# A two-layer model: the attention's fourth mask and context moved, its values projected once, two state-space projections moved, and another order at the end of the last feed-forward

## The chip, the cores and the metric

One core of one Trainium2 chip runs the whole program as one launch. The metric is the device time of one execution in microseconds (us), lower is better. TensorE is called PE here, its weight loads PEld; VectorE is DVE, ScalarE is ACT, GpSimd is POOL, and SyncE (SP) only issues DMAs.

## The reference

An input x of 2 sequences x 1024 tokens x 128 features passes through six blocks, each `x = x + block(layernorm(x))`, the feed-forwards with a factor 0.5 before the block:

1. a gated feed-forward (128 to 512 to 128, ReLU), scaled by the normalised top-two gates of 8;
2. windowed attention: 16 heads of 8 features, token i sees the tokens i-63 to i of its sequence; softmax over them, then an output projection with bias;
3. the gated feed-forward again;
4. a feed-forward with ternary weights and GELU, whose hidden rows are divided by their root mean square;
5. a selective state-space layer: in-projection to 2 x 256 channels, causal convolution over 4 tokens, SiLU, projections to delta, B and C, then for each channel and each of 16 states the recurrence h = exp(delta*a)*h + delta*u*B, y = sum of C*h, gated and projected out;
6. the ternary feed-forward again.

All data is fp32; a mask and some selector matrices are bf16.

## The kernel before, in words

Tokens are handled in 4 chunks of 512 (`NC`), each of 4 tiles of 128 (`TPC`), so 16 tiles (`NT`). Each engine runs a list of instructions written out by hand, in that order, and waits on counting semaphores. There is no planner: the order in the file is the order on the engine. The stages follow each other on the time axis: gated feed-forward (to 45 us), attention (45 to about 190 us), gated and ternary feed-forward (to about 262 us), state space (to about 500 us), ternary feed-forward `ter1` (to the end).

**Attention** (`attn_tensor`, `attn_vector`, `attn_scalar`). The heads are 4 groups of 4 (`j`). For tile t PE computes the scores of all four groups into four PSUM banks (`scores`, L683, 64 instructions). Each bank is first filled with the mask by a product with an identity (`mask_scores`, L671, one 512-column bf16 product), and the scores are added onto it. DVE takes each group's maximum (L566) and subtracts it (L571): that is `soften(t, j)`. ACT takes the exponent in place (`probs`, L836). PE transposes the four heads of the group (`prob_t`, L696). ACT copies the transposes out of PSUM (`probs_t`, L842), and PE multiplies them with the values (`values`, L710; the values carry a column of ones, so that the row sum comes with it). DVE divides by the row sum (`context`, L576 and L580), PE transposes the result (`context_t`, L736), ACT copies it (`copy_ctx`, L848), PE projects it (`project`, L740), and DVE adds it to x (`update`, L587). The work on tile t-1's context stands inside tile t. On PE one tile reads: transpose group 0, transpose the context of t-1, transpose group 1, project t-1, masks 0 and 1 of t+1, transpose group 2, masks 2 and 3, scores of t+1, values of groups 0 and 1, transpose group 3, values of groups 2 and 3.

The products of the next chunk are spread over tiles i = 1, 2, 3 of the chunk before: the transposes of x and the queries (L643, L648) in tile 1, the keys (L653) in tile 2. A window of the values begins every 64 tokens and is 128 tokens long, so each token's values are needed at two partition positions; the kernel projects them twice (`project_v(c, p)`, L663, eight instructions a call, two calls a chunk, one in tile 2 and one in tile 3), and ACT copies both (L830). For this, xw holds 64 tokens of the chunk before in front of the 512.

**State space** (`ssm2_*`). 64 steps k = 16 states x 4 units (sequence, half of the channels). In each step PE spreads B over the partitions (`spread_B`, L1173, into banks 2 and 3), DVE multiplies by delta*u (L1026), ACT makes exp(delta*a) (L1281), DVE runs the scan over 1024 tokens (L1047, three buffers hst), POOL multiplies with C (L1123, four buffers hC), and PE adds that onto y (`add_state`, L1193, five steps behind). Every fourth step (k % 4 = 3, but for the last one of units 1 and 2) POOL does DVE's product instead (L1107). `dt_proj(i)` (L1140) makes the delta of unit i; units 1 to 3 use banks 2 and 3, so nothing can be spread there until ACT has copied the result out (`take_z`). A softplus follows later, between two loads of ACT's function table.

**Ternary feed-forward** (`Ffn` ter0 and ter1). Per chunk: four up blocks (L441), GELU on each (L520), then four squares (L533), four down blocks (L447). POOL adds the four squares up (`ffn_pool`, L416 twice and L420), PE sums over the partitions (`token_sums`, L494, behind the up blocks of the next chunk, for the last chunk behind its own down blocks), DVE and POOL make the root (L375, L424, L380, L381) and DVE adds the scaled output to x (`update`, L389). The output leaves by one DMA a chunk.

## Time and profile before

| what | us |
|---|---|
| median of 3 timed executions | 553.44 (549.71 to 555.21) |
| the profiled execution | 548.81 |
| its span in the profile | 547.1 |
| PE busy | 476.1 (87%) |
| DVE busy | 440.7 (81%) |
| POOL busy | 305.2 (56%) |
| ACT busy | 273.0 (50%) |

The profile is one execution: 1.7 us lie around its span, and it stands 4.6 us under the median. Its times count from the start of the span. The granted clock (PEclk) is given as a share of 2.4 GHz, so 0.5 means 1.2 GHz. In a chain row a duration is the time by which the instruction moved the chain on.

### The profile page before, as it was taken

How to read it: one execution, taken by the hardware profiler on the slowest of the kernel's cores; microseconds unless marked ns; L12 is line 12 of the kernel's file. 1: busy time of each engine (PE TensorE's matmuls, PEld its weight loads, DVE VectorE, ACT ScalarE, POOL GpSimd, SP SyncE). 2: the span in 40 equal slices, each digit the busy share in tenths (PEclk: the TensorE clock that was granted, in tenths of full speed). 3: DMA queues.
4: the chain of work that ended last, by engine and by line, in shares of the span. 5: the costliest groups of instructions: out<-in, count | busy, mean ns of one | idle time of the engine just before them, and what ended most of it. 6: DMA issues, size and time to landing. Idle time of an engine off the chain costs nothing.

```text
span 547.1 us, 10120 instructions
## 1 busy us (share of the span) xinstructions
PE 476.1 (87%) x3876; PEld 290.8 (53%) x3876; DVE 440.7 (81%) x889; ACT 273.0 (50%) x420; POOL 305.2 (56%) x229
## 2 busy tenths in 40 slices
PE   7999899989899989999787889987667777889994
PEld 3876677777776777777331333333223233336764
DVE  4678768687769567667978988899999999998653
ACT  2345656565656524666786537344443434331742
POOL 3348200203000011567425888999999999993574
PEclk9999998999989899999896788989999998999998
DMA  8000000000000000000009843344553345100011
GB/s 218 5 0 3 4 2 1 2 3 4 1 2 3 2 0 2 2 0 2 0 31 416 340 154 154 143 166 166 218 230 155 154 192 206 62 1 0 2 39 40
DMA packets 12323, 42.74 MB, mean 78 GB/s; under 512 B 2858, under 2 KB 8755, under 8 KB 10227
## 3 DMA queue, kind: packets, MB, share of 16 engines
q1 hardware_dynamic: 11458, 41.56, 19.9%
q8 instruction: 31, 0.51, 0.4%
q10 hardware_dynamic: 816, 0.53, 0.3%
q14 instruction: 18, 0.14, 0.1%
HBM read 40.78 MB, written 1.31 MB: 77 GB/s over the span
## 4 chain that ended last, share of the span: by engine, by line
PE 44%; DVE 25%; issue 13%; POOL 8%; ACT 8%; DMA 1%; POOLq 0%; DVEq 0%; ACTq 0%
DVE hst L1047 10%; PE bk L447 6%; PE bk L441 6%; PE bk L710 5%; PE bk L696 5%; PE bk L1193 5%; PE bk L683 3%; ACT bk L1281 3%; DVE dBu L1026 3%; DVE xnT L278 3%; POOL hC L1123 3%; PE bk L671 2%; ACT g L842 2%; PE bk L931 2%; POOL powers L292 1%
## 5 line engine op out<-in xcount | busy, mean ns | idle before, releaser
L1123 POOL TENSOR_TENSOR hC<-hst,rows 128x1024 f32<-128x1024 f32 x62 | 144.7, 2359 | 14.8 <-DVE hst L1047 12.3
L1047 DVE TENSOR_TENSOR_SCAN hst<-bk,dBu 128x1024 f32<-128x1024 f32 x64 | 144.5, 2274 | 1.0 <-POOL dBu L1107 0.9
L1193 PE MATMUL bk<-hC,ident 128*128 128x512 f32 x256 | 127.6, 634 | 2.5 <-ACT ysb L1271 1.6
L1281 ACT ACTIVATE bk<-delta,aneg 128x1024 f32<-128x1024 f32 x64 | 71.5, 1118 | 100.2 <-DVE hst L1047 100.2
L285 POOL TENSOR_TENSOR veps<-mv,lneps 128x4 f32<-128x4 f32 x24 | 5.7, 239 | 159.2 <-DVE mv L257 159.1
L1193 PEld LDWEIGHTS bk<-hC,ident 128*128 128x128 f32 x256 | 51.3, 203 | 55.3 <-issue 41.5
L520 ACT ACTIVATE rows<-bk 128x512 f32<-128x512 f32 x64 | 38.1, 597 | 60.5 <-PE bk L441 60.5
L566 DVE TENSOR_REDUCE smax<-bk 128x4 f32<-128x512 f32 x64 | 43.7, 682 | 25.5 <-PE bk L683 25.5
L1026 DVE TENSOR_TENSOR dBu<-bk,du 128x1024 f32<-128x1024 f32 x50 | 59.9, 1198 | 5.2 <-PE bk L1173 5.2
L1173 PE MATMUL bk<-s,sel 96*128 96x512 bf16 x100 | 31.6, 398 | 35.7 <-DVE dBu L1026 33.3
L842 ACT COPY g<-bk 128x512 f32<-128x512 f32 x64 | 37.4, 585 | 47.0 <-PE bk L696 46.4
L1173 PEld LDWEIGHTS bk<-s,sel 96*128 96x128 bf16 x100 | 7.6, 100 | 74.1 <-DVE dBu L1026 58.3
L571 DVE TENSOR_TENSOR g<-bk,smax 128x512 f32<-128x512 f32 x64 | 44.2, 691 | 2.2
L836 ACT ACTIVATE g<-g 128x512 f32<-128x512 f32 x64 | 40.8, 638 | 8.4 <-DVE g L571 7.7
L696 PE MATMUL bk<-ident,g 128*128 128x128 f32 x256 | 42.2, 292 | 2.0 <-ACT g L836 2.0
L710 PE MATMUL bk<-rows,g 128*64 128x9 f32 x1024 | 38.1, 205 | 1.6
L710 PEld LDWEIGHTS bk<-rows,g 128*64 128x64 f32 x1024 | 33.7, 138 | 9.6 <-issue 5.1
L696 PEld LDWEIGHTS bk<-ident,g 128*128 128x128 f32 x256 | 31.1, 148 | 9.9 <-ACT g L836 5.1
L1107 POOL TENSOR_TENSOR dBu<-rows,du 128x1024 f32<-128x1024 f32 x14 | 33.0, 2357 | 0.0
L292 POOL TENSOR_TENSOR powers<-veps,lnpow 128x4 f32<-128x4 f32 (+1 forms) x24 | 30.1, 1255 | 1.9
L447 PE MATMUL bk<-wmoe,rows 128*128 128x128 f32 x256 | 30.3, 275 | 0.0
L441 PE MATMUL bk<-xnT,wmoe 128*128 128x512 f32 x64 | 30.2, 608 | 0.0
(174 smaller groups left out, 757.4 us busy)
## 6 DMA issues: line engine op xcount, KB each, us to landing
rows<-c_rows SPq DMA_DIRECT2D x16, 2048.0 KB, 7.1
rows<-c_rows SPq DMA_DIRECT2D x4, 1024.0 KB, 9.6
x<-in_x_dram SPq DMA_DIRECT2D x4, 256.0 KB, 4.9
out_dram<-x SPq DMA_DIRECT2D x4, 256.0 KB, 2.3
wmoe<-in_w_dram ACTq DMA_DIRECT2D x2, 256.0 KB, 5.3
wup<-in_upT_dram SPq DMA_DIRECT2D x1, 256.0 KB
wdn<-in_downT_dram SPq DMA_DIRECT2D x1, 256.0 KB
wproj<-in_in_wT_dram SPq DMA_DIRECT2D x1, 256.0 KB
```

What stands on the lines that cost most here:

```text
L441: nc.tensor.matmul(bank[k][:, :], f.w_up[:, k * P:(k + 1) * P], xT[:, :], start=True, stop=True).then_inc(f.up, 1)
L447: last = nc.tensor.matmul(psD[c % 2][:, i * P:(i + 1) * P], hT[:, k, i * P:(i + 1) * P], f.w_down[:, k, :], start=(k == 0 and i == 0), sto ...
L566: nc.vector.tensor_reduce(smax[:, j * HPG:(j + 1) * HPG], s3d, AX.X, ALU.max).then_inc(at["max"], 1)
L571: nc.vector.tensor_tensor(ssub[:, j, :].rearrange("p (a k) -> p a k", a=HPG), s3d, m, ALU.subtract).then_inc(at["sub"], 1)
L696: last = nc.tensor.transpose(psPT[j % 2][:, a * P:(a + 1) * P], ssub[:, j, a * P:(a + 1) * P], ident[:, :])
L710: last = nc.tensor.matmul(psO[64 * s:64 * s + 64, h, :], pT[:, j, a * P + 64 * s:a * P + 64 * s + 64], va[:, t // TPC % 2, 2 * (t % TPC) + ...
L842: nc.scalar.copy(pT[:, j, :], psPT[j % 2]).then_inc(at["pts"], 1)
L1026: nc.vector.tensor_tensor(dBu[k % 3][:, :], bk23[:, :], du[k // NS % 2][:, :], ALU.mult).then_inc(m2["dBu"], 1)
L1047: nc.vector.tensor_tensor_scan(hst[k % 3][:, :], dA[k % 2][:, :], dBu[k % 3][:, :], 0.0, ALU.mult, ALU.add).then_inc(m2["scan"], 1)
L1123: nc.gpsimd.tensor_tensor(hC[k % 4][:, :], hst[k % 3][:, :], crep[:, k % 12, :], ALU.mult).then_inc(m2["hC"], 1)
L1193: last = nc.tensor.matmul(bk01[:, r * CH:(r + 1) * CH], ident[:, :], hC[k % 4][:, r * CH:(r + 1) * CH], start=(k % NS == 0), stop=(k % NS ...
L1281: nc.scalar.activation(dA[k % 2][:, :], delta[:, i, :], ACT.Exp, scale=aneg[:, h * NS + n:h * NS + n + 1]).then_inc(m2["dA"], 1)
```

## The change

It has four parts.

**1. Order of the attention.** The mask of group 3 is multiplied in behind the scores (`mask_behind`, its own semaphore `masked`, which only DVE's group 3 waits for); the scores open that bank themselves. `scores` now waits for all four groups of the tile before. DVE's `context(t-1)` stands behind `soften(t, 2)` and not before it; on PE `context_t` stands behind masks 0 and 1, `project` behind the transposes of group 2; ACT's `copy_ctx` stands behind the exponent of group 2.

**2. Values once per token.** One `project_v(c)` and one copy a chunk write the odd windows of va; SP copies them by DMA from SBUF to SBUF into the even windows, two DMAs for chunks 0 and 2 and three for chunks 1 and 3, and `values` waits for them. xw loses its 64 tokens in front, with ACT's copy of them.

**3. Delta projections.** They stand at steps 0, 7, 19 and 27 instead of 0, 7, 11 and 15. For four steps behind each, `add_state` runs one step later, and is caught up with in step 11, 23 or 31. Softplus 2 moves from step 12 to step 28.

**4. End.** In both ternary feed-forwards each square follows its GELU, into two alternating buffers. For the last chunk of ter1 DVE adds the squares, not POOL, and PE takes the token sums before the last down block.

```diff
-        hsq = home(2048, KB, CH)
+        hsq2 = [home(2048, KB, CH), home(4608, KB, CH)]
...
+        def last_pair(dve, f, k):
+            hsq = hsq2[(NC - 1) % 2]
+            dve.wait_ge(f.hsq, (NC - 1) * KB + k + 2)
+            nc.vector.tensor_tensor(hsq[:, k, :], hsq[:, k, :], hsq[:, k + 1, :], ALU.add).then_inc(f.last, 1)
...
+        def shift_values(sp, c):
+            b = c % 2
+            sp.wait_ge(at["free"], 4 * c + 4)
+            sp.dma_start(va[64:128, b, 0:2 * TPC:2, :, :], va[0:64, b, 1:2 * TPC:2, :, :]).then_inc(v_shift[b], 16)
+            sp.dma_start(va[0:64, b, 2:2 * TPC:2, :, :], va[64:128, b, 1:2 * TPC - 1:2, :, :]).then_inc(v_shift[b], 16)
+            if b == 1:
+                sp.dma_start(va[0:64, b, 0:1, :, :], va[64:128, 0, 2 * TPC - 1:2 * TPC, :, :]).then_inc(v_shift[b], 16)
...
                 soften(t, 1)
+                soften(t, 2)
                 if t > 0:
                     context(t - 1)
-                soften(t, 2)
...
+                if t > 0:
+                    pe.wait_ge(at["sub"], t * JG)
-                pe.wait_ge(at["free"], 5 * c + 3)
+                pe.wait_ge(at["free"], 4 * c + 3)
...
                 last.then_inc(at["s"], 1)
+                mask_behind(t)
...
                 if ahead and i == 3:
-                    project_v(c + 1, 1)
+                    project_v(c + 1)
                 prob_t(t, 0)
-                if t > 0:
-                    context_t(t - 1)
                 prob_t(t, 1)
-                if t > 0:
-                    project(t - 1)
                 if t + 1 < NT:
                     mask_scores(t + 1, 0)
                     mask_scores(t + 1, 1)
                 if t == NT - 1:
                     expert_up(0)
+                if t > 0:
+                    context_t(t - 1)
                 prob_t(t, 2)
+                if t > 0:
+                    project(t - 1)
                 if ahead and i == 1:
                     project_q(c + 1)
-                if ahead and i == 2:
-                    project_v(c + 1, 0)
                 if t + 1 < NT:
                     mask_scores(t + 1, 2)
-                    mask_scores(t + 1, 3)
                     scores(t + 1)
...
+                probs(t, 2)
                 if t > 0:
                     copy_ctx(t - 1)
-                probs(t, 2)
...
+        Z_STEP = [0, 7, NS + 3, NS + 11]
...
+            def sums_to(k):
+                return max(0, k + 1 - LAG) - any(z <= k < z + 4 for z in Z_STEP[1:])
...
-                if k in (7, 11, 15):
-                    dt_proj(k // 4)
-                if k in (8, 12, 16):
-                    add_state(k - LAG - 1)
-                if k >= LAG and k not in (7, 11, 15):
-                    add_state(k - LAG)
+                if k in Z_STEP[1:]:
+                    dt_proj(Z_STEP.index(k))
+                for e in range(sums_to(k - 1), sums_to(k)):
+                    add_state(e)
...
                     if k == 12:
                         softplus(1)
+                    else:
                         softplus(2)
-                    else:
                         softplus(3)
...
                 for k in range(KB):
+                    if f is ter1 and c == NC - 1 and k == KB - 1:
+                        token_sums(c)
                     last = down_block(pe, f, c, k)
...
             for c in range(NC):
-                ffn_pool(pool, ter1, c)
+                if c < NC - 1:
+                    ffn_pool(pool, ter1, c)
```

In the last chunk's turn on DVE, the first `last_pair` stands before the mean of chunk 2, the second one and the total behind chunk 2's root and before chunk 2's update of x.

## Rows read from the trace of the kernel before

**Rows 1.** The attention as one stretch: length, busy of the engines (instructions), PEclk, DMA.

```profile
core 0: us, PE busy (x) PEld busy (x) DVE busy (x) ACT busy (x) POOL busy (x), PEclk, DMA share, GB/s
45.00:190.00 145.00, 133.52 (x2512) 103.39 (x2511) 109.24 (x241) 85.36 (x168) 27.64 (x27) 0.96 0.01 3
```

**Rows 2.** Chain that ended last, scores of tiles 9 to 14: start, us, what.

```profile
123.92 1.14 PE bk L683 x63
...
133.14 1.14 PE bk L683 x62
...
142.72 1.14 PE bk L683 x63
...
151.44 1.14 PE bk L683 x63
...
160.16 1.14 PE bk L683 x63
...
167.99 1.14 PE bk L683 x63
```

**Rows 3.** Timeline of tile 14: start, us, engine, line, operation [idle before].

```profile
172.11 0.26 DVE L576 RECIPROCAL rden<-bk 128x16 f32<-128x16 f32 x1 [0.21 <-PE bk L710]
...
172.61 0.68 DVE L566 TENSOR_REDUCE smax<-bk 128x4 f32<-128x512 f32 x1
172.69 0.59 ACT L842 COPY g<-bk 128x512 f32<-128x512 f32 x1
...
174.05 0.63 ACT L836 ACTIVATE g<-g 128x512 f32<-128x512 f32 x1 [0.61 <-DVE g L571]
...
174.65 0.69 DVE L571 TENSOR_TENSOR g<-bk,smax 128x512 f32<-128x512 f32 x1
174.73 0.42 PEld L696 LDWEIGHTS bk<-ident,g 128*128 128x128 f32 x4 [0.81 <-ACT g L836]
...
175.75 1.21 PE L683 MATMUL bk<-delta,rows 32*64 32x128 f32 x64
```

**Rows 4.** Chain through tiles 10 and 11: values, and values again.

```profile
141.40 0.89 PE bk L663 x8
...
146.79 1.09 PE bk L663 x8
```

**Rows 5.** A stretch of 5 us in tile 12, columns as in rows 1.

```profile
155.00:160.00 5.00, 4.90 (x35) 3.52 (x35) 3.67 (x8) 3.86 (x8) 0.00 (x0) 0.66 0.00 0
```

**Rows 6.** DMA issues: KB each, us to landing.

```profile
out_dram<-x SPq DMA_DIRECT2D x4, 256.0 KB, 2.3
```

**Rows 7.** Costliest groups on the page, then DVE's timeline in the first unit.

```profile
L1026 DVE TENSOR_TENSOR dBu<-bk,du 128x1024 f32<-128x1024 f32 x50 | 59.9, 1198 | 5.2 <-PE bk L1173 5.2
...
318.63 1.22 DVE L1026 TENSOR_TENSOR dBu<-bk,du 128x1024 f32<-128x1024 f32 x1 [1.80 <-PE bk L1173]
```

**Rows 8.** Timeline of the scan stage, PE in step 8, then POOL and DVE in unit 1.

```profile
312.87 5.29 PE L1193 MATMUL bk<-hC,ident 128*128 128x512 f32 x8
...
362.20 2.35 POOL L1123 TENSOR_TENSOR hC<-hst,rows 128x1024 f32<-128x1024 f32 x1 [0.54 <-DVE hst L1047]
...
378.35 2.36 POOL L1107 TENSOR_TENSOR dBu<-rows,du 128x1024 f32<-128x1024 f32 x1
...
380.76 2.28 DVE L1047 TENSOR_TENSOR_SCAN hst<-bk,dBu 128x1024 f32<-128x1024 f32 x1
```

**Rows 9.** Timeline of the last chunk of ter1.

```profile
531.96 0.60 ACT L520 ACTIVATE rows<-bk 128x512 f32<-128x512 f32 x1 [3.85 <-PE bk L441]
...
535.03 2.18 ACT L533 ACTIVATE rows<-rows 128x512 f32<-128x512 f32 x4
...
536.61 1.24 DVE L380 TENSOR_SCALAR gz<-gz 128x4 f32<-128x4 f32 x1 [1.13 <-POOL gz L424]
...
540.45 1.05 PE L494 MATMUL bk<-ones,rows 128*128 128x1 f32 x8 [1.49 <-POOL rows L420]
...
542.84 0.17 DVE L380 TENSOR_SCALAR gz<-gz 128x4 f32<-128x4 f32 x1 [1.13 <-POOL gz L424]
...
543.25 1.12 DVE L389 SCALAR_TENSOR_TENSOR x<-bk,gs,x 128x128 f32<-128x128 f32 x4
```

More of the change, by code:

```diff
@@ L171, in macaron_kernel @@
         out_done = sem("out_done")
+        v_shift = [sem(f"v_shift{q}") for q in range(2)]
         def layer_norm_semaphores(name, ternary=False):
@@ L198, in __init__ @@
                     self.sq = sem(name + "_sq")
+                    self.last = sem(name + "_last")
                     self.ssum = sem(name + "_ssum")
@@ L396, in ffn_vector @@
                     advance_two(dve, n, following, c)
+                    if f is ter1 and c == NC - 2:
+                        last_pair(dve, f, 0)
                     mean_square(c)
@@ L400, in ffn_vector @@
                     rms(c)
+                    if f is ter1 and c == NC - 2:
+                        last_pair(dve, f, 2)
+                        last_total(dve, f)
                 elif begun and c == 0:
@@ L411, in ffn_vector, with last_total @@
                     ternary_weights(dve, 0)
+        def last_pair(dve, f, k):
+            hsq = hsq2[(NC - 1) % 2]
+            dve.wait_ge(f.hsq, (NC - 1) * KB + k + 2)
+            nc.vector.tensor_tensor(hsq[:, k, :], hsq[:, k, :], hsq[:, k + 1, :], ALU.add).then_inc(f.last, 1)
+        def last_total(dve, f):
+            hsq = hsq2[(NC - 1) % 2]
+            dve.wait_ge(f.last, 2)
+            dve.wait_ge(f.ssq, NC - 1)
+            nc.vector.tensor_tensor(ssum[:, :], hsq[:, 0, :], hsq[:, 2, :], ALU.add).then_inc(f.ssum, 1)
         def ffn_pool(pool, f, c):
+            hsq = hsq2[c % 2]
             for k in range(0, KB, 2):
@@ L508, in ffn_tensor @@
                 ahead(pe)
-            if f.ternary:
+            if f is ter0:
                 token_sums(NC - 1)
@@ L527, in ffn_scalar @@
                     take_up(act, f, c, k)
-                if f.ternary:
-                    if c > 0:
-                        act.wait_ge(f.ssum, c)
-                    for k in range(KB):
+                    if f.ternary:
+                        if c > 1:
+                            act.wait_ge(f.ssum, c - 1)
                         act.wait_ge(f.h, c * KB + k + 1)
-                        nc.scalar.activation(hsq[:, k, :], hT[:, k, :], ACT.Square).then_inc(f.hsq, 1)
+                        nc.scalar.activation(hsq2[c % 2][:, k, :], hT[:, k, :], ACT.Square).then_inc(f.hsq, 1)
                 if c + 1 < NC:
@@ L626, in take_first @@
             act.wait_ge(at["xpose"], 1)
-            nc.scalar.copy(xw[:, 0, 64:64 + CH], psT).then_inc(at["free"], 1)
+            nc.scalar.copy(xw[:, 0, :], psT).then_inc(at["free"], 1)
         def attn_first(pe):
@@ L673, in mask_scores, with mask_behind @@
                                  start=True, stop=False, skip_group_check=True)
+            def mask_behind(t):
+                first = int(t % TPB == 0)
+                nc.tensor.matmul(bank[JG - 1][:, :].rearrange("p (a k) -> p a k", a=HPG), identb[:, :],
+                                 mask1[:, first:first + 1, :].to_broadcast([P, HPG, P]),
+                                 start=False, stop=True, skip_group_check=True).then_inc(at["masked"], 1)
             def scores(t):
                 c, b, r = t // TPC, t // TPB, t % TPB
-                pe.wait_ge(at["free"], 5 * c + 3)
+                if t > 0:
+                    pe.wait_ge(at["sub"], t * JG)
+                pe.wait_ge(at["free"], 4 * c + 3)
                 if c > 0:
@@ L685, in scores @@
                                                     kT[32 * j:32 * j + 32, b, r * P + 64 * s:r * P + 64 * s + P],
-                                                    start=False, stop=True, skip_group_check=True)
+                                                    start=(j == JG - 1 and a == 0), stop=(j < JG - 1), skip_group_check=True)
                 last.then_inc(at["s"], 1)
+                mask_behind(t)
             def prob_t(t, j):
@@ L742, in attn_tensor @@
             pe.wait_ge(set_attn, 1)
-            for j in range(JG):
-                if j == 3:
-                    pe.wait_ge(at["free"], 3)
+            for j in range(JG - 1):
                 mask_scores(0, j)
             scores(0)
-            project_v(0, 0)
-            project_v(0, 1)
+            project_v(0)
             for t in range(NT):
@@ L880, in attn_scalar @@
                     take_q(c + 1)
-                if ahead and i == 2:
-                    take_v(c + 1, 0)
                 if t == 0:
@@ L1308, in ssm2_scalar @@
                         softplus(1)
+                    else:
                         softplus(2)
-                    else:
                         softplus(3)
@@ L1363, in _ @@
                 sp.dma_start(dst, src).then_inc(w_in, 16)
+            for c in range(NC):
+                shift_values(sp, c)
             def rows_out(b):
```

81 lines of the change are left out of this document (38 added, 43 removed).

## The prediction

> **What bounds the kernel now.** I read the page's busy shares first (PE 87%, DVE 81%, in the table above): no engine bounds the whole. In the attention PE is busy for 133.5 of 145 us, DVE for 109, ACT for 85 [rows 1]. Then the chain that ended last. It runs over PE through the attention, over DVE's scans from 290 to 494 us, and over short steps that alternate between DVE, POOL and PE in the last 50 us. So each part of the change meets another bound, and I cost each in its own stage.
>
> In the attention the chain gives a tile's length, scores to scores: 9.22, 9.58 and 8.72 us for tiles 9, 10 and 11, which carry work of the next chunk, and 7.83 us for tile 13, which carries none [rows 2]. The timeline of tile 14, another without such work, tells why it isn't shorter: DVE takes the context of tile 13 (with a wait of 0.21 us) before group 2's maximum at 172.61; so ACT stands idle 0.61 us before group 2's exponent at 174.05, PE idles 0.81 us before the transposes at 174.73, and two masks later come the scores at 175.75 [rows 3]. In the scan stage DVE is dense but for 5.2 us of waits for PE's spread of B [rows 7]. At the end everything waits for POOL's last addition of squares [rows 9].
>
> **Attention, order.** The instructions stay, four masks a tile too; they move. Context costs DVE 0.50 us (172.11 to 172.61), and with its wait 0.7 us go from before group 2. The exponent can't use all of it: ACT copies group 0's transposes until 173.28 [rows 3], and the mask that now stands behind the scores pushes these transposes back by half of what two masks take, 0.2 us. So the exponent starts at 173.5 instead of 174.05. Then PE does group 2's transposes (174.2 to 174.6), the projection that has moved behind them (0.4), one mask (0.2), and the scores at 175.25: 0.5 us a tile. DVE's group 3, whose subtraction ended at 175.34 [rows 3], ends 0.3 us earlier and doesn't hold them up. What is late next is PE itself, without a gap from group 2's transposes on, so the fourth mask behind the scores gains nothing by itself: it leaves the path before the scores and enters that behind them. The bounds are 0 (the old chain over ACT holds) and 0.7 us (all that context took). Six tiles carry nothing of a next chunk (0, 4, 8, 12, 13, 14): 3.0 us.
>
> In tiles 1, 5 and 9 ACT also copies the transposed x and PE projects the queries; both stay, only the context's copy leaves the place before group 2's exponent. I take 0.2 us each, 0.6 us.
>
> **Attention, values.** In tiles 2, 6 and 10 PE projects the keys at the start and half of the values (0.89 us) just before the last masks, where the chain runs over it [rows 4]. The second leaves: 0.9 us each, 2.7 us. In tiles 3, 7 and 11 the other half, 1.09 us [rows 4], is replaced by the whole chunk's, again eight instructions; the new order gains little, since ACT's copy of the values and of group 0 stand before group 2's exponent: 0.1 us for the three. ACT loses four copies and two small ones, on no path.
>
> The price is ten DMAs from SBUF to SBUF, at most 144 KB each. The trace has none such. Its nearest row is the output's, 256 KB in pieces of 512 B: 2.3 us from issue to landing [rows 6]. Here the pieces are 576 B, three in a row at most, so 2.3 to 7 us. SP has nothing else to do in this stage. The first use, `values` of a chunk's first tile, stands behind the scores of its second tile: for chunk 0 some 4 us after ACT's copy (two DMAs, 2.3 to 4.6 us), for the others over 8 us. I take 0, and at most 1 us for chunk 0. Were they late, everything on PE behind `values` would wait, the next scores last.
>
> By the Trainium skill ("DMA: Bandwidth & Descriptors", section "Anatomy of one DMA") the fixed part is about 2.0 us, and these bytes add about 0.3 us at the rate it gives; the row of 2.3 us fits that, and the term stays 0.
>
> Attention: 3.0 + 0.6 + 2.7 + 0.1 = 6.4 us, between 0 and 9.
>
> **Delta projections.** Where one stands now, PE spreads B once and then catches up with two `add_state`, 8 instructions in 5.29 us [rows 8]; the next spread comes late and DVE waits 1.80 us at 318.63 [rows 7]. There are three such places, so about 3 us of the 5.2 are left for the two others; I take 1.8 and 1.2 us. After the change only one `add_state` follows in steps 8 and 9, and the two together fall in step 11, where POOL does the product and PE has no spread to make. I keep 0.3 us of the wait, since PE was at 1.2 GHz there (its first four instructions take about 3.4 us). So DVE gets 1.5 + 1.8 + 1.2 = 4.5 us ahead by step 17. POOL follows DVE only until step 12 and then works without a gap (product with C, next unit's delta*u, the product of step 15, and so on), so it gains the first two, 3.3 us, and falls 1.2 us back against DVE. This lag is the new wait: in step 20 POOL idled 0.54 us [rows 8], which takes up a part, but in step 27 POOL's product ended at 380.71 and the scan that needs it began at 380.76 [rows 8]. There DVE loses 1.2 - 0.54 - 0.05 = 0.6 us. Remaining: 4.5 - 0.6 = 3.9 us, which is POOL's pace.
>
> The projections at 19 and 27 stand where POOL does the product too, with the same catch-up, and I cost them at 0: the cover is a scan of 2.28 us [rows 8] on either side. If it is gone, each costs up to 1.8 us. Two softpluses now follow step 28, where one did; exponent 29 then comes later by one softplus, at most the 1.2 us that DVE needs for as many elements [rows 7]; two spread products and two scans of DVE lie between the exponents of 28 and the scan of 29, so 0 again. Scan stage: 3.9 us, between 0 and 5.2.
>
> **The ternary parts.** In ter0 and the first chunks of ter1, POOL starts on the squares only when its own roots are done, after the squares have ended; their interleaving and second buffer gain nothing. It costs nothing either: GELU 3 ends about 1.2 us later (two instructions of 0.6 us a block on ACT), still before the fourth down block. 0.
>
> In the last chunk GELU 0 starts at 531.96; four pairs of GELU (0.60) and square (2.18 / 4 = 0.55 [rows 9]) and 0.05 us between them end at 536.8, not 537.2. DVE makes the root of chunk 2 at 536.61. It took 1.24 us then, against 0.17 us at 542.84 when POOL added nothing [rows 9]; without POOL's additions I take 0.17. So the second addition starts at 537.1. An addition of 512 elements is half of L1026's 1.2 us [rows 7], so two take 1.3 us: the total is there at 538.45, where it was at 540.45 with PE's sums. PE is between down blocks 2 and 3 then. From the sums to the update it stays 543.25 - 540.45 = 2.8 us [rows 9]; the update starts at 541.3. The fourth down block (0.9 us) and chunk 2's update fit in between. 1.9 us, between 0.9 and 2.2.
>
> By the Trainium skill ("SBUF — State Buffer", section "Who interferes with whom") DVE and GpSimd share one pair of ports, which the first comer holds for its whole instruction. The row of 1.24 us agrees. If instead that instruction were simply slow there, the end would gain 0.9 us.
>
> **Sum.** 6.4 + 3.9 + 1.9 = 12.2 us. The profiled execution goes from 548.8 to 536.6 us. The median stands 4.6 us above it; on the median 553.4 - 12.2 = 541.2, and I predict 541 us.
>
> **Rivals.**
>
> *Forecast, 541 us (536.5 to 544.5).* Chance 0.54.
>
> *Attention held by ACT's queue.* PE waits for ACT in every tile; group 2's exponent now goes before the context's copy, so `project` and all behind it may wait for that copy. For it: 0.81 us of PE's idle time in tile 14 is ACT's [rows 3]. Against it: ACT is busy 59% of the attention [rows 1]. The order then gains 0 and the removed values stay: 2.7 for 6.4 us, 545 us. Chance 0.12.
>
> *The scan's waits only move.* PE's pieces now fall at steps 19 and 27, where DVE has no gap at all, and POOL's margin was 0.1 us. If each costs 1.8 us, the stage gains 0.3 us: 545 us. Chance 0.12.
>
> *The clock comes back.* The attention's mean clock of 0.96 [rows 1] means that PE had 1.2 GHz for some 12 us (145 x 0.04 / 0.5). Part of it lies in tile 12 (0.66 from 155 to 160 us, so 3.4 us of it) [rows 5], a bare tile that took 8.72 us, where tile 13 took 7.83 [rows 2]: 0.9 us for 3.4, about 2.5 for all, since some of it fell on PE's waits. Fewer gaps, no stretch: 2.5 us more, 538.5 us. The Trainium skill ("TensorE: Matmul & The Clock Gate", Part 1) has the throttled state as the default, which activity releases; that speaks for this case and against the next. Chance 0.15.
>
> *The clock goes: slower.* One mechanism: `values`, `context_t` and `project` now wait close together in PE's list, and if the clock falls there, PE has no slack left to hide it: each us at 1.2 GHz costs 0.5 us. Before, some 12 us ran so. From 25 us more on all 12.2 us are gone; 40 us more cost 20 us, and the time is 561 us. Against it: PE gets denser. Chance 0.07.
>
> **How the numbers follow.** The range, 534.5 to 547, holds the first four and the spread of the runs shown (5.5 us). A measurement of this kernel can tell about 1% from no change; 1% faster is 547.9 us, beyond the second and third case. Faster: 0.54 + 0.15 + most of 0.24 = 0.87; within 1%: 0.07; slower: 0.06.
>
> **What would show it.** Bare tiles of 7.3 us and tile 10 at 8.7 us; DVE's waits for the spread under 1 us in the first unit, one for POOL near step 27; PE's last token sums at 2 us after the last GELU's square, with a down block behind them. Wrong would be: `values` waiting on a DMA in more than the first tile, waits of DVE at steps 20 or 28, or bare tiles still near 7.8 us.

## The result, and the profile after

Against the kernel before in the same comparison the changed kernel took 544.64 us (541.96 to 549.32, 4 runs) for 554.33 (549.71 to 555.26, 4 runs): a ratio of 0.9891 with a 95% interval of [0.9842, 0.9940]. In the first round of experiments it was run again, 543.42 us for 551.68, ratio 0.9853 [0.9819, 0.9888]. So it is faster by 1.1 to 1.5%, 6 to 8 us, where 12.2 were forecast. The medians themselves lie 9.7 and 8.3 us apart; the text goes by the recorded ratios and their intervals.

The two profiled executions hardly differ, 549.32 us now for 548.81, and one thing has to be taken off before they are compared: the granted TensorE clock. Over the whole span its mean was 0.936 in this execution, 0.945 to 0.948 in the three others (541.96 to 544.76 us). The 23 later runs of the kernel before, one program, lie between 0.955 (548.72 us) and 0.937 (554.29 us): 0.01 of mean clock goes with some 3 us.

First the attention: windows of the changed kernel, columns as in rows 1, and the same stretch in the kernel with the attention's parts alone (second fence), which does the same work there.

```profile
45.00:190.00 145.00, 136.39 (x2473) 104.83 (x2474) 108.82 (x242) 81.78 (x165) 29.48 (x30) 0.92 0.04 10
350.00:355.00 5.00, 3.85 (x8) 1.57 (x7) 5.00 (x4) 3.15 (x3) 5.00 (x3) 0.65 1.01 383
355.00:360.00 5.00, 5.00 (x10) 1.72 (x9) 4.15 (x3) 0.27 (x1) 3.58 (x3) 0.67 0.09 36
530.00:535.00 5.00, 5.00 (x25) 4.13 (x25) 1.35 (x6) 0.57 (x1) 2.53 (x3) 0.76 0.17 52
```

```profile
45.00:190.00 145.00, 136.33 (x2542) 104.43 (x2540) 110.47 (x250) 83.88 (x168) 29.42 (x30) 0.98 0.04 10
```

0.92 and 0.98, where rows 1 have 0.96. The tiles show what that is worth. PE's timeline of the changed kernel, tile 4 and then tile 13, both bare (without work of a next chunk):

```profile
80.39 1.21 PE L719 MATMUL bk<-delta,rows 32*64 32x128 f32 x64
81.53 0.39 PE L705 MATMUL bk<-rows,identb 128*128 128x512 bf16 x1
81.84 1.10 PE L748 MATMUL bk<-rows,g 128*64 128x9 f32 x32
82.88 0.66 PE L733 MATMUL bk<-ident,g 128*128 128x128 f32 x4
83.47 1.38 PE L748 MATMUL bk<-rows,g 128*64 128x9 f32 x32
84.78 1.59 PE L733 MATMUL bk<-ident,g 128*128 128x128 f32 x8
86.17 1.06 PE L699 MATMUL bk<-rows,identb 128*128 128x512 bf16 x2
...
88.89 1.21 PE L719 MATMUL bk<-delta,rows 32*64 32x128 f32 x64
...
164.02 1.21 PE L719 MATMUL bk<-delta,rows 32*64 32x128 f32 x64
...
167.10 1.38 PE L748 MATMUL bk<-rows,g 128*64 128x9 f32 x32
168.41 1.13 PE L733 MATMUL bk<-ident,g 128*128 128x128 f32 x8
169.38 0.59 PE L699 MATMUL bk<-rows,identb 128*128 128x512 bf16 x2
...
171.30 1.21 PE L719 MATMUL bk<-delta,rows 32*64 32x128 f32 x64
```

Tile 13 takes 171.30 - 164.02 = 7.28 us, and PE's only idle time in it is 0.11 us; before it was 7.83 [rows 2]. Tile 4 takes 88.89 - 80.39 = 8.50 us: from 85 us on every product of PE takes nearly double (two masks 1.06 us for 0.59), for some 3.5 us. Seven tiles of this execution have such a stretch (4, 6, 7, 8, 10, 11, 12), each 1.2 to 1.4 us longer than its like at full clock. In the profile before there were two in the same tiles (4 and 12), for 0.74 and 0.89 us, and a third behind them, at 180.2 us. That ate the attention's gain in this profile: from the first scores to those of tile 15 it took 131.5 us for 130.2. All seven begin at the same place: as the second run of 32 products of nine columns ends (84.78 here). The number is that of one execution: six other profiles with the same order on PE have 2, 3, 3, 7, 8 and 9 stretches in the attention. The place is not: of the 61 stretches between 45 and 185 us in all 17 profiles, 60 begin within 0.45 us of the end of such a second run.

The transfers that shift the values, a group of DMA issues on the page (KB each, us to landing), and DVE's first wait in a tile:

```profile
rows<-rows SPq DMA_DIRECT2D x4, 144.0 KB, 2.5
...
rows<-rows SPq DMA_DIRECT2D x4, 108.0 KB, 2.3
```

```profile
L598 DVE TENSOR_REDUCE smax<-bk 128x4 f32<-128x512 f32 x64 | 43.6, 682 | 9.8 <-PE bk L719 9.7
```

Nobody waits for the transfers, and DVE's wait for the scores fell from 25.5 us to 9.7.

The scan stage. DVE's timeline: the first scan, two of the new waits, the last product with y (before, the last product began at 499.32 and the first scan at 292.24):

```profile
294.69 2.29 DVE L1075 TENSOR_TENSOR_SCAN hst<-bk,dBu 128x1024 f32<-128x1024 f32 x1
...
357.57 1.23 DVE L1054 TENSOR_TENSOR dBu<-bk,du 128x1024 f32<-128x1024 f32 x1 [0.85 <-PE bk L1201]
...
367.61 1.23 DVE L1054 TENSOR_TENSOR dBu<-bk,du 128x1024 f32<-128x1024 f32 x1 [1.12 <-PE bk L1201]
...
500.12 1.23 DVE L1097 TENSOR_TENSOR g<-bk,g 128x1024 f32<-128x1024 f32 x1 [1.12 <-PE bk L1221]
```

From the first scan to that last product it took 205.43 us for 207.08. The waits of rows 7 are gone (17th scan 50.9 us behind the first, for 55.5: 4.6 us ahead, 4.5 forecast), and a third new one of 0.63 us for POOL stands at 381.58, as forecast (0.6). The two above were not forecast. PE and ACT there:

```profile
349.15 1.95 PE L1168 MATMUL bk<-wmoe,wdt 9*128 9x512 f32 x4 [1.08 <-DVE dBu L1054]
...
352.25 1.01 PE L1201 MATMUL bk<-s,sel 96*128 96x512 bf16 x2 [1.15 <-issue]
353.06 3.62 PE L1221 MATMUL bk<-hC,ident 128*128 128x512 f32 x4
356.47 1.06 PE L1201 MATMUL bk<-s,sel 96*128 96x512 bf16 x2
357.32 2.37 PE L1221 MATMUL bk<-hC,ident 128*128 128x512 f32 x4
...
360.89 5.39 PE L1221 MATMUL bk<-hC,ident 128*128 128x512 f32 x12 [0.76 <-ACT ysb L1300]
```

```profile
359.73 1.01 ACT L1300 COPY ysb<-bk 128x1024 f32<-128x1024 f32 x1 [5.13 <-PE bk L1221]
```

Step 19 has the projection (1.95 us) between two idle times of 1.08 and 1.15 us; then PE is at 1.2 GHz for 7 us (0.65 and 0.67 in the windows above), an `add_state` takes 3.62 us for 1.88, the next spread is late, and the copy of y of unit 0 waits 5.13 us for the last sum, which now comes a step later. The wait of 1.12 us came at full clock: once y was copied, PE had three sums in a row (5.39 us from 360.89) and `add_skip` (1.02 us) ahead of the spread.

The end. Timeline of the last chunk, GELU and squares on ACT, root and second addition on DVE, sums on PE, update:

```profile
534.42 0.60 ACT L541 ACTIVATE rows<-bk 128x512 f32<-128x512 f32 x1 [5.48 <-PE bk L460]
...
538.74 0.63 ACT L553 ACTIVATE rows<-rows 128x512 f32<-128x512 f32 x1
```

```profile
539.08 0.17 DVE L382 TENSOR_SCALAR gz<-gz 128x4 f32<-128x4 f32 x1 [1.13 <-POOL gz L443]
...
539.49 0.69 DVE L423 TENSOR_TENSOR rows<-rows 128x512 f32<-128x512 f32 x1
540.22 0.69 DVE L429 TENSOR_TENSOR rows<-rows 128x512 f32<-128x512 f32 x1
...
543.76 1.13 DVE L391 SCALAR_TENSOR_TENSOR x<-bk,gs,x 128x128 f32<-128x128 f32 x4
```

```profile
540.96 1.05 PE L515 MATMUL bk<-ones,rows 128*128 128x1 f32 x8 [0.43 <-DVE rows L429]
```

From the first GELU to the update it is 543.76 - 534.42 = 9.34 us, for 543.25 - 531.96 = 11.29 [rows 9]: 1.95 us shorter, 1.9 forecast. Most of it doesn't show in the span because a stretch at 1.2 GHz fell on PE just ahead (0.76 in the last window), which cost 1.6 us: 32 products of the down blocks of chunk 2 took 5.37 us, for 3.74 in the kernel with the end alone. All 13 profiles with this part show 9.33 or 9.34 us from that GELU to the update, the other four 11.28 to 11.30; in six of the 13 the stage behind the last product with y is 1.6 us longer than in the seven others, as here.

### The profile page after: what moved, and what is told of

Read it like the earlier page. It is cut to its first block, busy times and chain, and to the rows that moved or that the text cites. A ratio compares the mean times of both kernels' runs of the same rounds, so it can differ in the third digit from the quotient of the medians.

```text
span 547.6 us, 10085 instructions
## 1 busy us (share of the span) xinstructions
PE 482.3 (88%) x3844; PEld 293.9 (54%) x3844; DVE 441.5 (81%) x892; ACT 268.8 (49%) x414; POOL 301.6 (55%) x225
## 4 chain that ended last, share of the span: by engine, by line
PE 45%; DVE 22%; issue 14%; POOL 10%; ACT 7%; DMA 1%; POOLq 0%; DVEq 0%; ACTq 0%
DVE hst L1075 8%; PE bk L466 6%; PE bk L733 6%; PE bk L460 6%; PE bk L748 5%; PE bk L1221 5%; POOL hC L1151 4%; PE bk L719 3%; DVE xnT L280 3%; ACT bk L1310 3%; DVE dBu L1054 3%; POOL powers L294 2%; ACT g L871 2%; DVE stats L255 1%; POOL dBu L1135 1%
## 5 line engine op out<-in xcount | busy, mean ns | idle before, releaser
L1221 PE MATMUL bk<-hC,ident 128*128 128x512 f32 x256 | 125.1, 623 | 2.7 <-ACT ysb L1300 1.8
L1201 PE MATMUL bk<-s,sel 96*128 96x512 bf16 x100 | 33.4, 419 | 33.3 <-DVE dBu L1054 30.7
L733 PE MATMUL bk<-ident,g 128*128 128x128 f32 x256 | 44.2, 313 | 7.0 <-ACT g L865 6.9
L733 PEld LDWEIGHTS bk<-ident,g 128*128 128x128 f32 x256 | 33.0, 159 | 16.0 <-ACT g L865 12.0
L865 ACT ACTIVATE g<-g 128x512 f32<-128x512 f32 x64 | 39.2, 636 | 1.3 <-DVE g L603 1.3
L466 PE MATMUL bk<-wdn,rows 128*128 128x128 f32 x256 | 31.8, 285 | 0.0
L460 PE MATMUL bk<-xnT,wmoe 128*128 128x512 f32 x64 | 31.6, 631 | 0.0
```

The lines of the kernel that those rows point to most:

```text
L460: nc.tensor.matmul(bank[k][:, :], f.w_up[:, k * P:(k + 1) * P], xT[:, :], start=True, stop=True).then_inc(f.up, 1)
L466: last = nc.tensor.matmul(psD[c % 2][:, i * P:(i + 1) * P], hT[:, k, i * P:(i + 1) * P], f.w_down[:, k, :], start=(k == 0 and i == 0), sto ...
L733: last = nc.tensor.transpose(psPT[j % 2][:, a * P:(a + 1) * P], ssub[:, j, a * P:(a + 1) * P], ident[:, :])
L1221: last = nc.tensor.matmul(bk01[:, r * CH:(r + 1) * CH], ident[:, :], hC[k % 4][:, r * CH:(r + 1) * CH], start=(k % NS == 0), stop=(k % NS ...
```

## The experiments

In the order in which they ran, but for the last two. There were four comparisons, each with its own runs of the kernel before (551.7, 553.5, 551.9 and 553.0 us), so ratios are what is compared.

**The changed kernel again.**

> The changed kernel again, unchanged. Theory A (clock): the edits do what the prediction said at 2.4 GHz, and the missing gain is TensorE time at 1.2 GHz (mean granted clock 0.936 in its profiled execution against 0.952 before) plus two new waits in the scan stage. Then its executions differ with the clock they were granted, about 0.5 us of time for each us at 1.2 GHz, and the median is 6 to 10 us under before (ratio 0.982 to 0.989). Theory B (the edits are worth half): the ratio is again 0.989 and doesn't follow the clock.

543.42 us, 0.9853 [0.9819, 0.9888]. The ratio is inside theory A's range, but the missing gain isn't the clock's: the mean clock of its runs is 0.946, for 0.947 in the 23 of the kernel before.

**Attention alone** (order, mask and values; the other hunks undone).

> Parts 1 and 2 alone (order of the attention, values once per token), scan stage and end as before. Theory A: bare tiles 7.3 us, tile kinds 1, 2, 3 of a chunk 9.05, 8.7 and 8.7 us at full clock, so 6.4 us less without clock losses, but more stretches at 1.2 GHz than before (7 against 3 in the profiled executions, each dearer than before: 1.2 us against 0.8), so 1 to 5 us faster than before (ratio 0.991 to 0.998). Theory B: tiles at full clock are no shorter than before in other executions, ratio 0.997 to 1.003.

545.13 us, 0.9891 [0.9857, 0.9926]: 6.0 us. In its profile thirteen of fifteen tiles are at full clock (5 and 6 aren't): 7.28 us bare, 9.07, 8.68 and 8.70 with work of a next chunk, to 0.05 us those of the changed kernel.

**Scan alone.**

> Part 3 alone (delta projections at steps 0, 7, 19, 27 with the delayed sums). Theory A: VectorE gains 4.6 us by step 16 and gives back 0.8 and 1.1 us in steps 20 to 24 (the y of unit 0 is handed over there, while the sums run one step late) and 0.6 us for GpSimd at step 27, so 2 us remain (ratio 0.996). Rival: the waits at steps 20 to 24 only came from a stretch at 1.2 GHz in that one execution, then 4 us remain (ratio 0.993).

553.97 us, 1.0047 [1.0018, 1.0075]: slower by 2.6 us, which neither had expected. The mean clock of its 12 runs is 0.940, for 0.947 in those of before beside them, so it ran 8 us longer at 1.2 GHz (552 x 0.0075 / 0.5). Windows of 350 to 400 us, this kernel and then the one before:

```profile
350.00:400.00 50.00, 43.22 (x99) 17.09 (x98) 47.15 (x28) 24.00 (x22) 47.51 (x22) 0.90 0.47 189
```

```profile
350.00:400.00 50.00, 38.91 (x96) 15.35 (x96) 50.00 (x31) 22.75 (x21) 48.91 (x23) 0.97 0.48 189
```

In this stretch the two profiles differ by 7 us at 1.2 GHz, and DVE, without a gap before, is idle for 2.85 of 50 us. But the changed kernel has the same stretches there (from 351.5 and 378.8 us) and its scan stage isn't longer for them (205.43 us), so they don't explain the 2.6 us.

**End alone.**

> Part 4 alone (squares between the GELUs, last squares added by VectorE, token sums before the last down block). Theory A: 1.9 us from the last up block to the end of the program at full clock (ratio 0.9965), unless a stretch at 1.2 GHz falls into the last chunk. Rival: the interleaved squares delay the GELUs and cost as much as they save (ratio 1.000, the last chunk no shorter).

550.76 us, 0.9973 [0.9944, 1.0002]: 1.5 us, with an interval that just reaches no change; 0.9852 below against 0.9891 above gives 2.2 us for the same part.

**All but the scan part.**

```diff
-        Z_STEP = [0, 7, NS + 3, NS + 11]
...
+                if k in (7, 11, 15):
+                    dt_proj(k // 4)
+                if k in (8, 12, 16):
+                    add_state(k - LAG - 1)
```

> The changed kernel with the delta projections put back to steps 7, 11 and 15 (parts 1, 2 and 4 stay). The kernel before took 551.7 us in the last comparison, the changed one 543.4. Theory 'given back': what DVE wins in unit 0 is lost again in steps 20 to 24, so the moved projections are worth nothing; the kernel without them takes 543 +- 1.5 us. Theory of the prediction: they are worth 3.9 us, and without them it takes 547 us or more. Theory 'the move lowers the clock': the moved projections alone made the time 0.5% longer at a lower mean clock (0.940 for 0.947); then the kernel without them is faster than the changed one, 541 us. Scores to scores of the bare tiles 7.3 us under each.

544.18 us, 0.9852 [0.9803, 0.9901], beside 0.9853 with it: worth nothing that these intervals could show. "Given back" holds, the 3.9 us don't, and neither do the 2 us by which the kernel was to be faster without the moved projections.

**Third projection at step 23, and at step 11.**

```diff
-        Z_STEP = [0, 7, NS + 3, NS + 11]
+        Z_STEP = [0, 7, NS + 7, NS + 11]
```

> The changed kernel with the third delta projection at step 23 instead of 19. Theory 'hand-over of y': the two DVE waits of 0.85 and 1.12 us after step 20 come because the sum of unit 0 is complete one step late (the projection has pushed add_state(15) behind step 20), so that ACT's copy of y holds the next decays and PE's next add_state; at step 23 there is no copy of y, both waits go, the stretch between the 17th and the 33rd scan takes 50.5 us for 52.5, and the kernel is 2 us faster than the changed one, 541.5 us. Rival 'PE has no room anywhere': the same waits come at steps 24 to 26; 543.5 us. Rival 'clock': the stretch at 1.2 GHz near step 20 stays and brings one wait of about 1 us; 542.5 us.

```diff
-        Z_STEP = [0, 7, NS + 3, NS + 11]
+        Z_STEP = [0, 7, 11, NS + 11]
```

> The changed kernel with the third delta projection at step 11, still in unit 0. Theory 'hand-over of y': as for the projection at step 23, the waits after step 20 go (2 us); step 11 has the catch-up of one add_state only, and the wait that stood there before (1.75 us) comes back at most in part, 0.3 us; 542 us. Rival 'any projection in unit 0 beside the one at 7 costs a full wait': 1.75 us come back, 543.3 us. Rival 'PE has no room anywhere': 543.5 us or more.

544.11 us, 0.9842 [0.9789, 0.9896], and 543.78 us, 0.9838 [0.9783, 0.9893]. Neither differs from the changed kernel, so the 2 us of the theory "hand-over of y" didn't come. The waits at the hand-over went, as it said, but others came. DVE and PE of the kernel with step 23:

```profile
373.02 1.22 DVE L1054 TENSOR_TENSOR dBu<-bk,du 128x1024 f32<-128x1024 f32 x1 [2.66 <-PE bk L1201]
```

```profile
366.13 1.95 PE L1168 MATMUL bk<-wmoe,wdt 9*128 9x512 f32 x4 [1.08 <-DVE dBu L1054]
368.01 3.68 PE L1221 MATMUL bk<-hC,ident 128*128 128x512 f32 x4
371.52 1.02 PE L1207 MATMUL bk<-u,diagD 128*128 128x512 f32 x2
```

Projection, `add_state` at 1.2 GHz, and `add_skip`, which has its place in that step: one wait of 2.66 us for two of 1.97. With step 11 it is the projection at 27 that meets 1.2 GHz, for waits of 0.92 and 0.40 us. The hand-over alone was not the cause.

**Order alone** (values projected twice per token as before).

> The kernel before with the new order of the attention and the mask behind the scores alone (values still projected twice per token, no shifting DMAs). Together with the values this took 6.5 us off (545.1 for 551.7). Theory of the prediction: the order is worth 3.6 us (0.5 in six bare tiles, 0.2 in three), 548.1 us, bare tiles of 7.3 us, tiles 2, 6 and 10 still 9.6 us. Rival 'order wants the freed PE': the half projection between the transposes of group 2 and the scores is on the path only without the order; then the order is worth 2 us, 549.7 us. Rival: all 6.5 us are the order's, 545 us, and the removed projection gives nothing.

547.33 us, 0.9909 [0.9868, 0.9950]: 5.0 us, with an interval that holds the 3.6. Its bare tiles take 7.28 us, its tile 2 9.57 us (9.58 before, 8.68 with the values' part): tile by tile the terms of 0.5 and 0.9 us are right.

**The mask between the values.** This follows from where the stretches begin.

```diff
                 last.then_inc(at["s"], 1)
-                mask_behind(t)
...
                 values(t, 1)
+                if t + 1 < NT:
+                    mask_behind(t + 1)
                 prob_t(t, 3)
```

> The changed kernel with the fourth group's mask not directly behind the scores but between the values and the transposes of group 3 (DVE needs it only some 4 us after the scores). The same instructions. Theory 'thin work calls the clock down': the stretches at 1.2 GHz in the attention begin behind the two runs of 32 products of nine columns each, and this puts a product of 512 columns between them; fewer stretches (mean granted clock of the attention 0.98 or more for 0.92, of a run 0.955 for 0.946), 541 us, 2.5 us faster than the changed kernel. Rival 'only the sum of work counts, not its place': the stretches stay at their number, 543.5 us. Rival 'DVE waits for the mask': bare tiles longer than 7.3 us and slower than 544 us.

538.59 us, 0.9781 [0.9739, 0.9824]: 4 us less than the changed kernel's 0.9853 would give, with the same instructions. Windows of the attention (45 to 180 us, where PEclk is 0.91 in the changed kernel), and PE's timeline of a bare tile:

```profile
45.00:180.00 135.00, 125.41 (x2454) 96.64 (x2454) 107.43 (x238) 80.22 (x162) 27.93 (x27) 0.97 0.04 11
```

```profile
153.05 1.21 PE L719 MATMUL bk<-delta,rows 32*64 32x128 f32 x64
154.19 1.10 PE L747 MATMUL bk<-rows,g 128*64 128x9 f32 x32
155.23 0.39 PE L705 MATMUL bk<-rows,identb 128*128 128x512 bf16 x1
155.46 0.60 PE L732 MATMUL bk<-ident,g 128*128 128x128 f32 x4
155.99 1.38 PE L747 MATMUL bk<-rows,g 128*64 128x9 f32 x32
...
160.22 1.21 PE L719 MATMUL bk<-delta,rows 32*64 32x128 f32 x64
```

Two stretches (at 65.6 and 164.6 us), and mean clocks of 0.948 to 0.957 in its runs. One profile against one proves little, since the kernel with the attention alone had only two as well. All of them together tell more: with the mask directly behind the scores the eight profiles have 7, 9, 2, 3, 3, 7, 3 and 8 stretches in the attention, with it between the values the four have 2, 1, 3 and 0. Tiles at full clock got shorter too, 7.17 us for 7.28 here: the mask holds PE 0.23 us (155.23 to 155.46) where it held it 0.31 (81.53 to 81.84). The kernels' sums over fifteen tiles at full clock are 120.9 and 122.6 us, so 1.7 us come from that; the rest I put down to the clock, whose mean over the runs is 0.953 here and 0.946 in the changed kernel.

**A second mask moved up as well.**

```diff
                 values(t, 2)
+                if t + 2 < NT:
+                    mask_scores(t + 2, 0)
                 values(t, 3)
```

> As the mask between the values, and the first group's mask of the tile after next also moved up, to between the last two runs of values. Theory 'thin work': no stretch at 1.2 GHz between tiles 1 and 15, 540.5 us. Rival 'only the sum counts': 543.5 us. Rival 'PE waits for DVE's subtraction of group 0': 0.3 us a tile, 546 us or more.

539.56 us, 0.9796 [0.9754, 0.9838]. No stretch at all in the attention's window, the same line as above:

```profile
45.00:180.00 135.00, 123.48 (x2459) 95.36 (x2458) 107.80 (x239) 81.28 (x164) 28.92 (x30) 1.00 0.04 11
```

Its tiles are those of the changed kernel at full clock again (7.28 us), so it isn't faster than the kernel with one mask. With one mask there is a profile without a stretch too (the variant with the sum ahead of the projection at 7, 11 and 15, below).

**Two products that nobody needs.**

```diff
+                if j == 3:
+                    for _ in range(2):
+                        nc.tensor.matmul(psPT[1][:, :].rearrange("p (a k) -> p a k", a=HPG), identb[:, :],
+                                         mask1[:, 0:1, :].to_broadcast([P, HPG, P]), start=True, stop=True)
```

> The changed kernel with two more products of 512 columns a tile, ahead of the transposes of group 3, into a bank that these overwrite (nothing of the result changes). They cost PE 2 x 0.21 us a tile: bare tiles 7.7 us for 7.28, 6.7 us for sixteen tiles at full clock. Theory 'thin work': no stretch in the attention; its mean granted clock 0.99, that of a run 0.965 for 0.946, which gives back some 5 us: 545 us. Rival 'the stretches have nothing to do with the thin products': clock as before, 550 us.

545.26 us, 0.9900 [0.9858, 0.9942], no stretch in the attention either, mean clocks up to 0.961. Tiles of 7.67 us (bare) add 5.4 us in all; the time rose by 2.6 (0.9900 for 0.9853), so work that serves only the clock gave back about half of its price. Not tested is whether the width of such a product matters or only that something stands between the two runs.

**Nothing held back in unit 1.**

```diff
-                return max(0, k + 1 - LAG) - any(z <= k < z + 4 for z in Z_STEP[1:])
+                return max(0, k + 1 - LAG) - any(z <= k < z + 4 for z in Z_STEP[1:2])
```

> The changed kernel with the sums of y held back only behind the projection at step 7, not behind those at 19 and 27, where add_state now follows at once while ACT copies the projection's result (PE idled 1.15 us there). Theory: the hand-over of y comes a step earlier, so the DVE waits of 0.85 and 1.12 us after step 20 go and one of 0.5 us for the spread of step 20 comes; the stretch at 1.2 GHz that began in PE's idle time at step 19 is 3.5 us for 7; 1.5 us faster than the changed kernel, 542 us. Rival 'PE has no room in unit 1': the waits stay at 2 us in sum, 543.5 us. Rival: the clock falls behind each projection whatever follows, and add_state at 1.2 GHz ahead of the spread costs DVE 2.5 us, 544.5 us.

544.76 us, 0.9877 [0.9828, 0.9927]. The stretch at step 19 was 3.4 us for 7, as the theory said, but it met the `add_state` ahead of the spread (3.35 us), and DVE waited 1.80 and 0.96 us: the last rival, with 2.8 us where it said 2.5. It is right for the first of the two waits only: no stretch follows the projection at step 27, and the 0.96 us came at full clock, with the projection, an `add_state` and `add_skip` ahead of the spread.

**The sum ahead of the projection,** on the kernel with the mask between the values, at steps 7, 19, 27 and then at 7, 11, 15.

```diff
-                if k in Z_STEP[1:]:
-                    dt_proj(Z_STEP.index(k))
                 for e in range(sums_to(k - 1), sums_to(k)):
                     add_state(e)
+                if k in Z_STEP[1:]:
+                    dt_proj(Z_STEP.index(k))
```

> The kernel with the fourth group's mask between the values (538.6 us), and in the scan stage nothing held back: in the steps with a projection (7, 19, 27) add_state runs first, in the 1.08 us in which PE idled there, then the projection. Theory 'catch-up': the cost was the sums held back and caught up with behind the projection; now the projection ends 0.65 us later, the spread of the next step with it, and DVE waits at most 0.3 us at each of the three places (for 0.85, 1.12 and 0.63 at 20 to 27): first to 33rd scan 101.5 us for 103.5, 537 us. Rival 'PE has no room in unit 1 in any order': the waits there stay at 2 us in sum, 538.6 us. Rival 'clock': a stretch at 1.2 GHz still follows each projection and now meets the spread and the sum behind it, 1 us each, 538.5 us, but with the waits directly behind the projections.

> As the kernel with add_state ahead of the projection, with the projections at 7, 11 and 15, where they stood before the change. Theory 'catch-up': these places never cost by themselves, the two sums behind them did; DVE's waits for the spread in unit 0 are under 1 us (for some 3 to 5 us in the kernel before), and none comes at 20 to 28; 536.5 us. Rival 'PE has no room beside a projection': 1 us at each, 539 us.

540.36 us, 0.9786 [0.9747, 0.9826], and 541.39 us, 0.9807 [0.9764, 0.9850]: no gain over 0.9781, where "catch-up" had 537 and 536.5 us. DVE in the first of them, step 8:

```profile
309.67 1.23 DVE L1056 TENSOR_TENSOR dBu<-bk,du 128x1024 f32<-128x1024 f32 x1 [1.80 <-PE bk L1203]
```

After step 19 it waits 0.52 us, but 1.80 at step 8, as much as the catch-up cost before the change, in a stretch at 1.2 GHz (from 308.9 us). In the second kernel DVE's waits in unit 0 sum to 4.7 us, as in the profile that the prediction read; stretches follow two of its projections (307.4 and 321.0 us), but behind the third DVE waits 1.18 us (at 334.78) at full clock. "Catch-up" falls as the whole cause: PE is short beside a projection in either order, and the clock adds to it.

**The mask between the values, scan part undone.**

> The kernel with the mask between the values (538.6 us) and the delta projections back at steps 7, 11 and 15 with their old catch-up. Theory 'the move is worth nothing': 538.6 +- 1 us. The prediction's 3.9 us: 542.5 us. Rival 'the move costs, as it did alone (2.3 us)': 536.5 us.

538.66 us, 0.9765 [0.9726, 0.9805]: once more the move is worth nothing. It is the lowest ratio of the study, though it can't be told from 0.9781: 13 us under the kernel before and some 5 under the changed one. DVE's waits for the spread in its first unit, behind one of 0.43 us at 301.67:

```profile
310.91 1.23 DVE L1054 TENSOR_TENSOR dBu<-bk,du 128x1024 f32<-128x1024 f32 x1 [0.32 <-PE bk L1201]
...
324.75 1.22 DVE L1054 TENSOR_TENSOR dBu<-bk,du 128x1024 f32<-128x1024 f32 x1 [1.59 <-PE bk L1201]
```

**The scan stage in all profiles.** With the projections at 7, 11 and 15, the first scan to the last product with y took 207.08 us in the profile that the prediction read, and 205.79, 205.84, 206.26, 205.14 and 205.32 in the five other kernels with that code (order, attention, end, all but scan, mask without scan): 205.9 in the mean of all six. At 7, 19 and 27 with the sums held back it took 205.43, 205.49, 205.59, 205.33, 204.78 and 205.92: 205.4. So 0.5 us, not 3.9. Of the five other variants the projection at step 11 had the shortest stage (204.55 us, its ratio no better for it), step 23 took 205.77, nothing held back in unit 1 205.47, and the two with the sum ahead of the projection 206.20 and 207.03 us.

## Why the prediction was wrong in size

The direction and the range held; the gain was 6 to 8 us for 12.2. The profiles give 6.1 us for the attention, 0.5 for the scan stage and 1.95 for the end, 8.5 in all, so the term that was wrong is the scan stage's. By the steps:

**Attention, 6.4 us: right.** Bare tiles 7.28 (7.3 forecast), tile 2 8.68, tile 10 8.7 where the clock was full, tiles 1, 5, 9 gained 0.15 (0.2), tiles 3, 7, 11 nothing (0.1). Tile 0 gained 0.2 us, not 0.5: it has no context ahead of group 2's maximum. Five bare tiles times 0.55, 0.2, three times 0.15 and three times 0.9 make 6.1 us at full clock; alone the parts took 6.0 us off, by the ratio. The transfers cost nothing (2.5 us to landing, no wait). "Held by ACT's queue" is refuted by the bare tiles; in the tiles with work of a next chunk PE does still wait 0.7 us for ACT's exponent, where the clock is full.

**End, 1.9 us: right.** 1.95 by the timeline, 1.5 alone in the median. The root took 0.17 us without POOL's additions at its side; the step that named a lock on the ports as its reason has this row for it and no further test.

**Scan, 3.9 us: the step that failed, for two reasons.** The prediction read 5.2 us of waits in one execution and took them for the code's. They were the clock's as well: in that profile all three projections of unit 0 were followed by a stretch at 1.2 GHz (from 313.4, 327.0 and 340.7 us), in the five other profiles of the same code one of three each, and DVE's waits for the spread in unit 0 that are over 0.3 us sum to 2.2 to 3.3 us instead of 4.7. So 1.5 to 2.5 of the 4.5 us weren't there to be won in a usual execution. And "the projections at 19 and 27 cost 0" was wrong: at 19 the stage gave back 0.85 us, for a spread at 1.2 GHz, and 1.12 us, for the sums that had piled up behind the hand-over of y. The 17th scan began 55.5 us behind the first in the profile that was read, 53.0 to 54.1 in the five others and 50.9 in the changed kernel; the 16 steps from there took 49.6, 50.2 and 52.5 us. The prediction had no term for the projection's own effect on the clock, although it wrote down that PE was at 1.2 GHz in step 8. The forecast wait for POOL (0.63 us) came at its place, but all five other profiles with the projections at 7, 11 and 15 have one of 0.50 to 0.53 us at that scan already, and only the profile that was read had none: the price came out right by luck, since most of it was no new cost. The rival "the scan's waits only move", at 0.12, is what happened, and its 545 us were nearer than the forecast's 541.

**The clock.** The two rivals on it asked about the attention's mean. In the profiled execution it fell from 0.96 to 0.92, for four more stretches of 1.2 to 1.4 us each; in the kernel with the attention alone it rose to 0.98. Of the medians it took next to nothing, the mean clock of the runs being 0.947 before and 0.946 after in the larger comparison. But the prediction stopped one question short: it had a stretch in tile 12 [rows 5] and didn't ask what PE did just ahead of it. Acting on that answer was worth more (4 to 5 us) than the whole scan part.

**Open.** Alone the scan part made the kernel 2.6 us slower; on top of the rest it cost nothing (0.9853 and 0.9852, 0.9781 and 0.9765). Its own stage was shorter than before even then (205.59 us), so the loss lies elsewhere. In its profile all the rest is longer than in the one before, though the code there is the same: 47.35 us for 45.52 to the first scores, 132.63 for 130.23 to those of tile 15, 118.05 for 116.49 to the first scan, 49.36 for 47.77 behind the last product with y, with 39 us at 1.2 GHz in these four for 25. The lower clock goes with the loss in all its runs, but why a change in a late stage should bring it on isn't shown. Nor is it shown what in a projection makes PE short beside it in either order: that a stretch at 1.2 GHz began within 4.5 us of its start in 27 of 51 cases (17 profiles, three projections each) is a count, not a test.

## What to carry to other kernels

A wait read in one execution is a term of the sum only if the granted clock at that place is the usual one: look at the window around each wait that the gain is built on, and take off what a stretch at 1.2 GHz made. Where the engine that feeds the bound (here PE for DVE) is short for a step, moving the extra work to another step moves the wait. And if the clock falls at the same place of a loop again and again, put a wide product that has slack into the thin stretch ahead of it: moving one mask of 512 columns between two runs of nine-column products gave 4 to 5 us for nothing, more than either of the two smaller parts of the change.

## What the runs showed of the hardware

- The stretches at 1.2 GHz in the attention come without idle time on PE: in the 4 us ahead of each of the 61 it is idle for 0.11 us (once 0.21), and tile 4, which has one, and tile 13, which has none, have the same work and the same 0.11 us. They depend on what PE does ahead of them, though not on that alone. With 64 thin products (nine columns each) and four transposes between, eight profiles had 2 to 9 of them; with one product of 512 columns moved in among these, four profiles had 0 to 3; with a second mask moved up as well, or two products added, none, in one profile each. The Trainium skill ("TensorE: Matmul & The Clock Gate", Part 1) ties the throttled state to a PE that has been idle, and the prediction took that as speaking against a slower clock; the trace of tile 4 differs, since PE is idle there for only 0.11 us. The measurement decides.
- The stretches come in runs: in the changed kernel at 102.3, 112.5, 122.8 and at 139.8, 150.1, 160.3 us, each 10.2 us behind the last, in tiles of 10.0 and 9.9 us. Whether one brings the next on isn't shown.
- Executions of one program differ in mean clock by up to 0.018 (0.937 to 0.955 in 23 of the kernel before), with some 3 us of time per 0.01; most of the spread between runs of this kernel is that.
- A shift of 144 KB from SBUF to SBUF, half of the partitions to the other half in pieces of 576 B, takes 2.5 us from issue to landing, little more than the 2.3 us of 108 KB.
- The same mask of 512 columns holds PE for 0.31 us directly behind the scores' 32-row products and 0.23 us behind the nine-column ones.
